# A state-space mixer on one core: the order of a slot's work on TensorE turned, with fixed PSUM banks and the tanh of projection tiles in PSUM

## The reference, cut to what matters

```python
xn = _layernorm(x)
proj = einsum('bsd,ed->bse', xn, in_proj_w)          # gate 8192, hBC 10240, dt 128
hBC = silu(depthwise_conv4(hBC) + conv_b)            # hs: 128 heads of 64; Bm, Cm: 8 groups of 128
xch = hs * dt
Y_diag = einsum('bzlhn,bzshn,bhzls,bzshp->bzlhp', Cc, Bc, L, xch)      # inside a chunk of 128 tokens
states = einsum('bzlhn,bhzl,bzlhp->bzhpn', Bc, decay_states, xch)
Y_off = einsum('bzlhn,bzhpn,bhzl->bzlhp', Cc, prev, exp(A_cum))        # from the state before the chunk
g = (Y_diag + Y_off + hs * D) * silu(gate)
out = (g * rsqrt(mean_over_1024(g * g) + EPS)) * norm_w
return x + out @ out_proj_w.T + base(xn) + lora_experts(xn)
```

## Time and profile before

| | |
|---|---|
| median of 3 runs | 1799.87 us (1796.86 to 1800.7) |
| the profiled execution's own time | 1797.44 us |
| its span, first to last instruction | 1796.1 us |
| TensorE busy | 1688.6 us, 94% |
| VectorE busy | 1381.9 us, 77% |
| ScalarE busy | 1246.5 us, 69% |
| GpSimd busy | 1082.6 us, 60% |

### The profile page before, as it was taken

The page is one execution under the profiler, slowest core; times in us unless marked ns, Lnnn a source line. Parts: engine busy times, 40 slices in busy tenths (PEclk is TensorE's granted clock), DMA queues, the critical chain, the costliest instruction groups (busy, mean ns, idle before and its releaser), DMA issues.

```text
span 1796.1 us, 32206 instructions
## 1 busy us (share of the span) xinstructions
PE 1688.6 (94%) x11244; PEld 1355.8 (75%) x11244; DVE 1381.9 (77%) x1793; ACT 1246.5 (69%) x2687; POOL 1082.6 (60%) x1037
## 2 busy tenths in 40 slices
PE   6979999999999999999999999999999999999988
PEld 4767777787777877778777777778777787777766
DVE  6768778886887878887778877887687877878765
ACT  5167676776767777676776777777667777677775
POOL 3036467665676656665567556765566755776575
PEclk9989999999999999999999999999999999999999
DMA  3242143332433234332333324342343323433142
GB/s 122 91 148 93 62 145 127 120 108 88 133 124 120 86 101 143 120 124 75 131 120 135 98 78 151 112 142 87 100 133 116 130 76 103 143 124 104 65 141 95
DMA packets 97167, 202.57 MB, mean 113 GB/s; under 512 B 28392, under 2 KB 29936, under 8 KB 92784
## 3 DMA queue, kind: packets, MB, share of 16 engines
q1 hardware_dynamic: 97008, 200.51, 33.6%
HBM read 162.20 MB, written 38.28 MB: 112 GB/s over the span
## 4 chain that ended last, share of the span: by engine, by line
PE 68%; DVE 16%; POOL 6%; ACT 5%; issue 5%; DMA 0%; DVEq 0%; ACTq 0%; SPq 0%; POOLq 0%
PE P L241 20%; PE P L243 19%; PE P L242 18%; DVE hsX L641 5%; PE P L400 5%; POOL GL L884 4%; DVE hsX L647 2%; PE P L287 2%; PE P L417 2%; DVE Bx L641 1%; ACT P L475 1%; DVE P L846 1%; DVE yb L849 1%; DVE EM L682 1%; POOL yb L932 1%
## 5 line engine op out<-in xcount | busy, mean ns | idle before, releaser
L932 POOL TENSOR_TENSOR yb<-yb,dhs 128x512 f32<-128x512 f32 x112 | 144.2, 1287 | 412.0 <-DVE yb L824 412.0
L475 ACT ACTIVATE P<-AB,SC 128x128 f32<-128x128 f32 x1024 | 308.7, 370 | 0.0
L241 PE MATMUL P<-xh,AH 128*128 128x512 f32 x656 | 270.2, 412 | 37.8 <-DVE hsX L641 32.3
L641 DVE SCALAR_TENSOR_TENSOR hsX<-P,cwt,hsX 128x1023 f32<-128x1023 f32 (+2 forms) x192 | 245.5, 1279 | 18.1 <-ACT hsX L441 13.6
L243 PE MATMUL P<-xh,AL 128*128 128x512 f32 x656 | 257.4, 392 | 0.0
L242 PE MATMUL P<-xl,AH 128*128 128x512 f32 x656 | 257.2, 392 | 0.0
L618 ACT ACTIVATE tg<-P 128x512 f32<-128x512 f32 x127 | 76.0, 598 | 255.2 <-PE P L243 255.2
L241 PE MATMUL P<-GH,xh 128*128 128x512 f32 x544 | 220.7, 406 | 16.2 <-POOL GL L884 16.2
L241 PE MATMUL P<-OH,gTh 128*128 128x512 f32 x512 | 213.8, 418 | 2.3 <-issue 2.2
L243 PE MATMUL P<-GH,xl 128*128 128x512 f32 x544 | 214.0, 393 | 0.0
L242 PE MATMUL P<-GL,xh 128*128 128x512 f32 x544 | 213.7, 393 | 0.0
(11 more groups left out here) (181 smaller groups left out, 4067.7 us busy)
## 6 DMA issues: line engine op xcount, KB each, us to landing
AB<-acr_d SPq DMA_DIRECT2D x128, 512.0 KB, 4.9
AR<-in_wa SPq DMA_DIRECT2D x80, 256.0 KB, 2.8
TS<-in_wg SPq DMA_DIRECT2D x16, 1024.0 KB, 5.0
TS<-in_wo SPq DMA_DIRECT2D x16, 1024.0 KB, 5.4
part_d<-pl SPq DMA_DIRECT2D x64, 256.0 KB, 3.2
pl<-part_d SPq DMA_DIRECT2D x64, 256.0 KB, 2.7
al<-acc_d SPq DMA_DIRECT2D x64, 256.0 KB, 3.0
acc_d<-al SPq DMA_DIRECT2D x58, 256.0 KB, 2.2
```

The costliest lines, as they stand in the source:

```text
L241: te.matmul(o, ah_, bh_, start=(first and i == 0), stop=False)
L475: r = se.activation(E[:, h, :], AB[m % 2][:, h, :], ACT.Relu, bias=SC[s % 2][:, c, 3, h:h + 1], scale=-1.0)
L641: ve.scalar_tensor_tensor(out=o[:, d:T], in0=raw[:, 0:T - d], scalar=cwt[:, n, 3 - d:4 - d], in1=o[:, d:T], op0=ALU.mult, op1=ALU.add).the ...
L932: pe_.tensor_tensor(yb[:, :], yb[:, :], dhs[:, :], ALU.add).then_inc(s_tp, 1)
```

## The change

Six things are changed together:

1. TensorE's slot now runs Off, St, Y of slot m, then T and BG of slot m+1, A, O of slot m-1, GTr of slot m, GT of slot m+1. Before, it ran T, BG, A, Off, St, Y, O, GT, GTr.
2. The rotation over banks 5, 6 and 7 is gone. Off and T share bank 5, St and O bank 6, Y and GTr bank 7, BG and GT bank 4.
3. The tanh of a tile is written over the raw tile in PSUM (banks of A) and no longer to `th` in SBUF. The banks of A are so freed by the SiLU (semaphore xs) and not by the convolution, and the first decay waits for the SiLU of six tiles.
4. ScalarE's list: the decay of slot m+1 first, then SH, hsr, sq, DH, the tap of a finished tile, pl, gTh, the tile's tanh, and `tg` last. At a layer's last chunk GH comes ahead of all. `tg` came before gTh.
5. VectorE's list: t1 and S first, then the gate, Y's sum and g, then xch, dxh and EM of slot m+1, the convolution, al, gTl, and the SiLU of the same tile last. The convolution and the SiLU of the tile before it followed g. OL moves from the end of chunk 0 to chunk 1 between g and xch.
6. GpSimd's list: SL and the state's decay first, then dhs, CL, and DL last.

```diff
-            jobs += [in_turn("T", m + 1)]
-            jobs += [in_turn("BG", m + 1)] if (m + 1) // 8 % 2 == 0 else []
+            jobs += ([("Off", m, (5,))] if c else []) + ([("St", m, (6,))] if c != 7 else []) + [("Y", m, (7,))]
+            jobs += [("T", m + 1, (5,))] + ([("BG", m + 1, (4,))] if (m + 1) // 8 % 2 == 0 else [])
...
-            "LA": lambda u: [(s_mid, u + 1)], "LGt": lambda i: [(s_lg, 1)], "A": lambda i: [(s_conv, 3 * i + 3)],
+            "LA": lambda u: [(s_mid, u + 1)], "LGt": lambda i: [(s_lg, 1)], "A": lambda i: [(s_x, i + 1)],
...
-            se.activation(th[:, :], tile_out(i), ACT.Tanh).then_inc(s_th, 1)
+            se.activation(pair("A", i), tile_out(i), ACT.Tanh).then_inc(s_th, 1)
...
-                se.wait_ge(s_conv, 18)
+                se.wait_ge(s_x, 6)
...
-            ve.scalar_tensor_tensor(out=o, in0=th[:, :], scalar=1.0, in1=o, op0=ALU.add, op1=ALU.mult).then_inc(s_x, 1)
+            ve.scalar_tensor_tensor(out=o, in0=pair("A", i), scalar=1.0, in1=o, op0=ALU.add, op1=ALU.mult).then_inc(s_x, 1)
...
+                if m + 1 < M:
+                    dve_front(m + 1)
+                    dve_decay(m + 1)
+                for i in done:
+                    dve_conv(i)
...
+                for i in done:
+                    dve_silu(i)
```

More of the change, by code:

```diff
@@ L53, in mamba_moe_block_kernel @@
     jobs += [("F", i, (4 + i % 4,)) for i in range(4, 8)] + [("A", 2, (0, 1))] + [("SC", c, (4 + c % 4,)) for c in range(8)]
[L54 to L59, removed]
+    jobs += [("A", 3, (2, 3)), ("A", 4, (0, 1)), ("A", 5, (2, 3)), ("T", 0, (5,)), ("BG", 0, (4,)), ("GT", 0, (4,))]
     for k in slot_halves[0]:
@@ L402, in pe_program @@
                     r.then_inc(s_y, 1)
+                if m + 1 < M:
+                    pe_front(m + 1)
+                if m < M:
+                    for k in slot_halves[m + 1]:
+                        pe_half(k)
                 if m:
@@ L588, in act_program @@
                 done = [k // 2 for k in slot_halves[m + 1] if k % 2] if m < M else []
+                if c == 7 and s + 1 < NS:
+                    se.wait_ge(s_gt, m + 1)
+                    act_gate_hi(s + 1)
                 if m + 1 < M:
+                    act_decay(m + 1)
+                    act_state_hi(m + 1)
                     act_front(m + 1)
[L591 to L598, removed]
                 if m < M:
@@ L627, in act_program @@
                             se.activation(OH[:, j, :], TS[:, j, :], ACT.Copy, scale=nwt[:, 4 * s + j:4 * s + j + 1]).then_inc(s_oh, 1)
-                    for i in done:
-                        act_ring(i + 4)
-                        act_tanh(i)
+                for i in done:
+                    act_ring(i + 4)
+                    act_tanh(i)
+                if m + 1 < M:
+                    se.wait_ge(s_gt, m + 2)
+                    se.activation(tg[:, :], bank("GT", m + 1), ACT.Tanh, scale=0.5).then_inc(s_tg, 1)
         def dve_conv(i):
@@ L814, in dve_program @@
                 pm, pc, ps = m - 1, (m - 1) % 8, (m - 1) // 8
[L815 to L816 removed]
+                done = [k // 2 for k in slot_halves[m + 1] if k % 2] if m < M else []
                 if m < M:
[L818 removed]
                     o = bank("St", m) if c != 7 else None
@@ L849, in dve_program @@
                     ve.tensor_tensor(yb[:, :], bank("Y", m), tg[:, :], ALU.mult).then_inc(s_g, 1)
[L850 to L855, removed]
+                    if c == 1:
+                        for j in range(4):
+                            ve.wait_ge(s_oh, 4 * s + j + 1)
+                            ve.scalar_tensor_tensor(out=OL[:, j, :], in0=TS[:, j, :], scalar=nwt[:, 4 * s + j:4 * s + j + 1],
+                                                    in1=as_f(OH[:, j, :]), op0=ALU.mult, op1=ALU.subtract).then_inc(s_ol, 1)
+                if m + 1 < M:
+                    dve_front(m + 1)
+                    dve_decay(m + 1)
+                for i in done:
+                    dve_conv(i)
                 if m and ps % 2:
```

48 lines of the change are left out of this document (22 added, 26 removed).

## The result

The changed kernel takes 1872.78 us (median of 4 runs, 1869.09 to 1878.65), the kernel before 1800.14 beside it: a ratio of 1.041 (95% interval 1.0379 to 1.0442). The forecast was 1833 with a range from 1788 to 1860. The direction was right. The size, +73 us instead of +33, was not.

A forecast was written before the change was run, and what follows sets the result against it. TensorE, busy 94% of the span, was taken as the bound. Start +12, slots 0 to 15 0, six pairs +25, slots 112 to 117 +6 and tail -10 gave +33: 1833 us, range 1788 to 1860.

The forecast's parts named there:

- OL's price and reach: Slot 1: four OL taking 3.56 us ahead of xch cost TensorE 1.4 us in odd layers, 3.8 in even ones.
- this stage: Slots 16 to 111, six layer pairs: each pair 4.2 us slower at 215.7 us, together +25 us.
- The start: Ahead of the loop: tiles 4 and 5 wait for SiLUs, first T at 131.0 instead of 119.18 us, +12 us.
- Slots 0 to 15: First two layers: five finished tiles in layer 0, coming out even, 0 us.
- The tile chain: Slots finishing a tile: tap, convolution, SiLU and t1 end late, holding T, St and BG; 15.5 us per pair in eight waits.
- The SiLU from PSUM: VectorE's SiLU with its tanh in PSUM: 1.3 us instead of a median of 1.99, bounds 1.2 and 2.0.
- GL: Layer ends: the 16.2 us of TensorE's waits for the split of the gate's weights go.
- DL: Last in GpSimd's list: ready by 10.8 us, wanted by St at 12.4; free unless operations stretch by more than 1.6 us.
- The tail: Slots 118 to 127, without projections: 9.0 us each instead of 10.03, together -10 us.
- Slower still: Rival, chance 0.22: SiLU stays near 2.0 us or GpSimd's stretching makes DL or SL hold St or Off; 1855 to 1871.
- Faster: Rival, chance 0.13: t1 comes in time, seven of ten waits vanish, a pair takes 204.9 us; 1756 us.

The follow-up runs named there:

- e10_pool_waits: Changed kernel with GpSimd starting SL, the state's decay and dhs in chunk 1 only when the four OL are done: 1821.76 us, ratio 1.0132.
- e5_th_sbuf: Changed kernel with every tile's tanh in SBUF, A's banks freed by the convolution, the first decay not waiting for the SiLUs: 1883.2 us, ratio 1.0451.
- e3_start_back: Changed kernel with the first six tiles as before (tanh in SBUF, banks freed by the convolution) and slot 0's BG in bank 6: 1851.04 us, ratio 1.0287.
- e4_silu_later: Changed kernel with a tile's SiLU moved behind t1 and the gate of the next slot: 1854.04 us, ratio 1.0301.
- e2_al_first: Changed kernel with al ahead of the convolution in slots 1 and 7 of odd layers: 1875.94 us, ratio 1.0432.
- e12_best_silu: Changed kernel with GpSimd waiting for OL, first six tiles as before, SiLU behind next slot's t1 and, in even layers, its gate: 1772.97 us, ratio 0.9843.
- e9_rotation: Changed kernel with the new order of products but the old rotation over banks 5, 6 and 7: 1846.19 us, ratio 1.0252.

## Why the prediction was wrong, point by point

**The step that failed is OL's price and reach**: "Slot 1 starts late on VectorE and holds the four OL (3.56) ahead of xch, so al and SiLU end late though it is a double: 1.4", and "Even layer: behind slot 1, with OL ahead of xch, t1 ends at 17.6: 3.0 and 0.8 for BG, 3.8". The duration was taken from the old place, behind gTl, though the change moves GpSimd's SL, state decay and dhs beside OL. In the trace after it is 5.2 to 5.4. Its reach was cut short too: the prediction followed OL to t1 in even layers, but O of the slot before reads OL (waits of 0.50 and 0.48 us), Y waits for gTl behind it (1.55), and St behind slot 1 of odd layers waits for al (2.7 us, in the same way as behind slot 7, where I had it). In even layers T waits 1.17 us for t1 and not 3.0. Per pair that is +3.8 in the even period 1 to 2 and +2.8 in the odd one, with -2.3 over all others: +4.3, times six +26, which is the miss of this stage (50.6 against 25). e10_pool_waits shows that the contention alone accounts for 51 us of the whole, lower clock behind the waits included, which is more than the miss of 40. Part of it was in the forecast: 3.56 is 0.8 above the 2.73 of four OL alone, and 5.23 is 1.7 above 3.56. Over 16 layers the part left out is some 27 us, by my estimate.

The prediction held the rule that explains it. The Trainium skill, SBUF — State Buffer, section Who interferes with whom, says that a VectorE instruction with two SBUF inputs contends with a GpSimd instruction that reads SBUF. I weighed it for the SiLU, whose operand leaves SBUF, and the traces agree (1.61 in e5_th_sbuf, 1.22 after). OL has both TS and OH in SBUF, and I did not ask it of OL: 0.744 alone, 1.536 in company, the traces agree again. By the rule the slow rows were also the warning: a form that spreads from 1.2 to 2.3 has a price that depends on its neighbour.

**The start** was mis-sized: the first T at 134.35 and not 131.0, the first Y 16.6 us later and not 12. By e3_start_back the tanh in PSUM and the bank of BG cost 20 to 22 there, of which the turned order hides some 4. That tiles 4 and 5 wait for SiLUs was right (6.4 us each, some 6 said). What the sum lacked is the clock, 2 us per tile, and a wait of GT for Gt through BG in its bank:

```profile
140.24 0.80 PE L235 MATMUL P<-GH,xh 128*128 128x512 f32 x1 [4.17 <-DVE Gt L673]
```

**The clock** was no term of the sum at all. Over the span it fell from 0.991 to 0.975. Eight Ys run wholly or mostly at the lower level, none before, seven of them 0.8 us longer and one 0.6, and with slower neighbours. Seven follow a wait of St for al, one the wait for DL.

**Slots 0 to 15** (+2.9 for 0) have OL's contention in both layers: the stage takes 212.2 in e10_pool_waits.

**The tile chain** was right in place, and its waits were at or under the forecast. T waits 1.17 behind slot 0 of odd layers (1.8 said), T 0.52 and BG 0.54 behind slots 3 and 5 of even ones (1.5 said for both), and al holds St behind slot 7 by 2.94 (3.1 said). Behind slot 4 of odd layers T waited 0.28, and St 0.34 for al (1.1 said). e4_silu_later removes the waits of T and BG for 19 us, and e2_al_first shows them and those for al to be one queue.

**The SiLU from PSUM** takes 1.22 (1.3 said). **GL** no longer holds GT (0.2 us in all), and **DL** last on GpSimd cost one wait of 1.36 us in the whole run.

**The tail** brought 3.5 us, not 10. The pace of the last layer, from 1809.78 on, is the 9.0 that was forecast. Slots 119 to 121 lost the rest, to DL and then to OL:

```profile
1796.00 1.15 PE L390 MATMUL P<-xch,EM 128*64 128x64 f32 x32
1799.82 0.47 PE L235 MATMUL P<-OH,gTh 128*128 128x512 f32 x1 [2.07 <-DVE OL L848]
1801.41 0.50 PE L235 MATMUL P<-OH,gTh 128*128 128x512 f32 x1 [0.68 <-DVE OL L848]
...
1809.78 1.15 PE L390 MATMUL P<-xch,EM 128*64 128x64 f32 x32
1818.85 1.15 PE L390 MATMUL P<-xch,EM 128*64 128x64 f32 x32
```

**The rivals.** "Slower still" named GpSimd's list stretching until DL or SL holds TensorE. The contention was real, but it was VectorE's OL that stretched; so this rival had the right pair of engines and the wrong victim, and its 1855 to 1871 ended just under the result. "Faster" fell with the waits at t1, though e12_best_silu shows that the new order with OL undisturbed, the start kept and the SiLU moved is 28 us faster than the kernel before. What these mends would give in the old order was not tried, so how much of the 28 us is the order's own stays open.

**What stays open.** How e9_rotation's 27 us divide between BG and the looser St was not tried by itself. How much of the 51 us of e10_pool_waits is OL's duration and how much the clock is not separated either: 16 layers by 5.23 - 2.73 = 2.5 us would be 40 for the first, and leave 11 for the second, if all of OL's time reached TensorE.

## What to carry to other kernels

When a change moves an instruction, take its duration from rows that had the new neighbours and not from its old place; where an operation reads only SBUF and another engine's list moves beside it, price it at its slow row. Follow a late result to all its readers in the order of the waiting engine's list, since removing the first wait (al, 41.9 us) gave nothing while the work ahead of it stayed. And before an order is thrown away, hold one engine back by one wait: here it cost nothing that TensorE waited for and gave 51 us.

## What the runs showed of the hardware that I had not expected

- VectorE's scalar_tensor_tensor of 128x512 with both tensors in SBUF took 0.744 us alone and 1.536 in the median (1.79 at most) beside GpSimd's tensor_tensor on SBUF. Over the span VectorE lost 41 us by it (64 x 1.385 = 88.6 against 64 x 0.744 = 47.6), GpSimd 16 (busy 1036.7 after, 1020.5 in e10_pool_waits).
- Behind both gaps of 6.38 us TensorE had a granted clock of 0.50 (104.9 to 109.4 us) and 0.51 (119.1 to 123.1), with 0.43 us from one matmul to the next, and then 1.00, with 0.227. Waits of 2.67 to 2.94 us had the same effect in some slots and not in others of the same kind: behind 2.71 us for al the Y of slot 74 was slow and that of slot 26 was not.
- The lower level also came behind shorter waits. In slots 18 and 34, of the same kind, Y waited about 1.5 us for gTl and T 1.17 for t1; behind them the clock was 1.00 in one and 0.50 in the other, and the period 2 to 3 took 14.0 and 16.3 us:

```profile
397.00:401.00 4.00, 3.35 (x18) 2.72 (x19) 3.52 (x7) 3.97 (x11) 2.58 (x2) 1.00 0.41 143
...
616.00:620.00 4.00, 3.92 (x13) 2.94 (x12) 3.52 (x7) 3.59 (x9) 2.60 (x3) 0.50 0.42 133
```
